# Two neighbouring blocks' short float32 products issued as one pair on the two column halves of TensorE

## What is computed

```python
x = _layernorm(x + _L0_gnn_ref(x, edge_index, ...), axis=-1)       # passes 0 and 1
# _L1_gnn_ref, passes 2 to 4:
def _mp_layer(x, src_f, dst_f, ea_f, W, b):
    m = jnp.concatenate([x[dst_f], x[src_f], ea_f], axis=1) @ W.T + b
    agg = jax.ops.segment_sum(m, dst_f, num_segments=n)
    return jax.nn.relu(agg)
h = _mp_layer(x, src_f, dst_f, ea_f, W0, b0)
h = jax.nn.relu(_batchnorm(h, g0, be0))
h = _mp_layer(h, src_f, dst_f, ea_f, W1, b1)
h = jax.nn.relu(_batchnorm(h, g1, be1))
h = _mp_layer(h, src_f, dst_f, ea_f, W2, b2)
x = _layernorm(x + h, axis=-1)
```

## Time and profile before

| | |
|---|---|
| median of 3 runs | 1153.56 us (1153.36 to 1153.74) |
| span of the profiled execution | 1151.4 us; its own time is not recorded apart, and the median lies 2.2 us above the span |
| TensorE busy (PE) | 973.9 us, 85% of the span |
| DVE busy | 718.9 us, 62% |
| ScalarE busy | 391.3 us, 34% |
| passes 2 to 4 | from 645.3 us to the end of the span |

### The profile page before, as it was taken

How to read it: one execution, slowest core, us unless ns; L and a number is a source line. 1 busy time by engine, 2 the same in 40 slices (tenths; PEclk the granted TensorE clock), 3 DMA queues, 4 the chain that set the end, 5 groups by cost and what they waited for, 6 DMA issues and landing times. The chain is left out here.

```text
span 1151.4 us, 19166 instructions
## 1 busy us (share of the span) xinstructions
PE 973.9 (85%) x7566; PEld 582.8 (51%) x7566; DVE 718.9 (62%) x1328; ACT 391.3 (34%) x750; POOL 131.4 (11%) x150
## 2 busy tenths in 40 slices
PE   0247877978688778999999999998999998999993
PEld 0246776868677665545555444443433443444441
DVE  5797989999999943623434755553465554334434
ACT  2485688887877720200000010213320104110000
POOL 4022223343222320000000000000000000000001
PEclk9868988989888977999999999998999998999997
DMA  6325546656545439953775435755036755037740
GB/s 165 57 74 206 177 130 242 199 177 195 174 125 181 177 127 292 377 235 140 317 278 211 183 120 234 276 219 224 15 126 249 286 192 224 19 147 280 286 173 23
DMA packets 63701, 216.77 MB, mean 188 GB/s; under 512 B 28320, under 2 KB 41627, under 8 KB 50067
## 3 DMA queue, kind: packets, MB, share of 16 engines
q1 hardware_dynamic: 55588, 164.52, 39.7%
q0 software_dynamic: 8016, 50.95, 12.3%
HBM read 170.69 MB, written 44.74 MB: 187 GB/s over the span
## 5 line engine op out<-in xcount | busy, mean ns | idle before, releaser
L1382 PE MATMUL PM<-Aring,Xop 128*128 128x512 fp8e4 (+1 forms) x1960 | 398.5, 363 | 0.0
L1382 PEld LDWEIGHTS PM<-Aring,Xop 128*128 128x128 f16 x1960 | 181.4, 98 | 216.7 <-issue 16.3
L821 PE MATMUL PW<-Aring 128*128 128x52 fp8e4 (+3 forms) x2151 | 120.9, 220 | 66.5 <-ACT F L889 64.0
L1907 ACT ACTIVATE F<-PH,bag 64x512 f32<-64x512 f32 (+1 forms) x39 | 25.5, 658 | 370.3 <-PE PH L1601 370.2
L821 PEld LDWEIGHTS PW<-Aring 128*128 128x128 fp8e4 x2151 | 114.8, 105 | 70.7 <-ACT F L889 66.5
L1382 PE MATMUL PM<-Ares,Xop 128*128 128x512 fp8e4 x588 | 138.1, 390 | 2.7 <-ACT Xop L1946 1.3
L1740 DVE TENSOR_SCALAR S<-PM 128x256 f32<-128x256 f32 (+1 forms) x75 | 31.4, 418 | 112.7 <-PE PM L1382 95.8
L1382 PEld LDWEIGHTS PM<-Ares,Xop 128*128 128x128 f16 x588 | 56.2, 100 | 71.7 <-issue 9.8
L1531 POOL DMA_DIRECT2D out<-dd x12 | 9.0, 754 | 705.8 <-DVE dd L1702 705.8
L889 ACT ACTIVATE F<-PW 128x392 uint16<-128x392 f32 x196 | 84.6, 513 | 11.0 <-PE PW L821 9.6
L679 DVE TENSOR_TENSOR Aring<-Ares 128x4096 uint16<-128x4096 uint16 x31 | 70.8, 2285 | 6.4 <-PE PW L821 6.1
(11 more groups left out here) (158 smaller groups left out, 1233.0 us busy)
## 6 DMA issues: line engine op xcount, KB each, us to landing
Aring<-adj SPq DMA_DIRECT2D x72, 1568.0 KB, 9.6
adj<-Aring POOLq DMA_DIRECT2D x12, 1568.0 KB, 5.9
adj<-Xop POOLq DMA_DIRECT2D x12, 1568.0 KB, 6.3
Ares<-adj SPq DMA_DIRECT2D x6, 1568.0 KB, 21.4
rc<-ea_sum SPq DMA_DIRECT2D x36, 128.0 KB, 5.7
Aring<-adj SPq DMA_DIRECT2D x4, 784.0 KB, 4.4
rc<-rc_d SPq DMA_DIRECT2D x12, 256.0 KB, 9.5
eaf<-in_erow SPq DMA_DIRECT2D x60, 51.0 KB, 2.0
```

What stands on the lines that cost most here:

```text
L821: last = nc.tensor.matmul(PW[begun % RING][:, c:c + 52 * (z - y)].rearrange("p (d v b) -> p d v b", d=z - y, b=2), lo[:, h % 2, i, :].bitc ...
L1382: last = nc.tensor.matmul(o, x[:, h, :], rhs, start=h == 0, stop=h == NT - 1)
L1907: nc.scalar.activation(F[0:64, c:c + w], PH[b % 2][0:64, 0:w], ACT.Relu, bias=t["bag"][:, 4 + conv:5 + conv]).then_inc(s_hr, 1)
```

## The change

In passes 2 to 4, `post(b)` of an even block does nothing (except the last, block 12), and `post(b)` of an odd block issues the short products of both, b-1 and b: first the two `ws` products, then the two `wc` products. The even block's output lies in partitions 0 to 63, the odd block's in 64 to 127 of one PSUM tensor, `PH[b // 2 % 2]`, so that the first uses TensorE's columns 0 to 63 and the second 64 to 127. ScalarE reads its half. In pass 4 the transposes follow three blocks behind instead of two, and ScalarE's `root(b-2)` stands ahead of the Relu of an even block. DVE, SP and GpSimd have the code that they had.

```diff
+        def halves(b):
+            return PH[b // 2 % 2][64 * (b % 2):64 * (b % 2) + 64, 0:blk(b)]
+
         def post(b):
             n, c = blk(b), b * 512
+            if p >= 2 and b % 2 == 0 and b < NB - 1:
+                return
             pe.wait_ge(s_S, b + 1)
             if p >= 2:
                 pe.wait_ge(s_r, b + 1)
...
             else:
-                if b >= 2:
-                    pe.wait_ge(s_hr, b - 1)
-                o = PH[b % 2][0:64, 0:n]
-                nc.tensor.matmul(o, m["ws"][conv][:], S[:, b % 2, 0:n], start=True, stop=False)
-                nc.tensor.matmul(o, m["wc"][conv][:], F[0:97, c:c + n], start=False, stop=True).then_inc(s_h, 1)
+                couple = [x for x in (b - 1, b) if x // 2 == b // 2]
+                if couple[0] >= 4:
+                    pe.wait_ge(s_hr, couple[0] - 2)
+                for x in couple:
+                    nc.tensor.matmul(halves(x), m["ws"][conv][:], S[:, x % 2, 0:blk(x)], start=True, stop=False)
+                for x in couple:
+                    nc.tensor.matmul(halves(x), m["wc"][conv][:], F[0:97, x * 512:x * 512 + blk(x)], start=False,
+                                     stop=True).then_inc(s_h, 1)
...
-        for i in range(NB + 2):
+        behind = 3 if p == 4 else 2
+        for i in range(NB + behind):
...
-            if i >= 2:
-                post2(i - 2)
+            if i >= behind:
+                post2(i - behind)
...
             else:
+                if p == 4 and b % 2 == 0 and 2 <= b < NB - 1:
+                    act.wait_ge(s_a, b - 1)
+                    root(b - 2)
                 act.wait_ge(s_h, b + 1)
-                nc.scalar.activation(F[0:64, c:c + w], PH[b % 2][0:64, 0:w], ACT.Relu,
+                nc.scalar.activation(F[0:64, c:c + w], PH[b // 2 % 2][64 * (b % 2):64 * (b % 2) + 64, 0:w], ACT.Relu,
                                      bias=t["bag"][:, 4 + conv:5 + conv]).then_inc(s_hr, 1)
-                if p == 4 and b >= 2:
+                if p == 4 and b >= 2 and (b % 2 or b == NB - 1):
                     act.wait_ge(s_a, b - 1)
                     root(b - 2)
```

## The result

The changed kernel takes 1180.74 us (1177.03 to 1181.79, 4 runs), the kernel before 1153.46: ratio 1.0228, 95% interval 1.0213 to 1.0243. The forecast was 1182.4, slower. The profiled execution took 1181.43 us, its span 1177.5. One execution each of the kernel before, of e10 and of e11 took far longer (1337, 1667 and 2556 us); the medians and ratios in this text leave them out.

The account below looks back on a forecast made before the run. TensorE bounds the kernel, with 1.8 us of slack for ring loads. Pass 2 +32.9, pass 3 -1.4, pass 4 -2.7 make +28.8 on the 1151.4 span: 1180.2, or 1182.4 by the median; range 1171 to 1206.

Parts of the forecast that it names:

- The move: Even blocks' products issued one main product later, so in pass 2 their check cannot begin under their own main product.
- The stalls: Pass 2: TensorE waits 8.7 us for ring loads ahead of blocks 6, 8 and 10; +22.3 us over the three.
- T_4: End of block 4's main product in a pass; in pass 2 no stall was forecast before it.
- The clock: Pass 2: lower clock behind each stall costs 2.2 us, +6.6 for three, and 1.0 more at the pass's end.
- The pair: Two blocks' short products on separate column halves take 2.28 us instead of 3.72, saving 1.44 where TensorE is the bound.
- instructions start in order: Within a pair, column halves overlap but starts keep program order: five slots instead of eight, 2.28 us.
- rival 5: Pair takes four slots, 1.86 us, 0.42 less than forecast: 4.6 us less in all, 1178; chance 0.18.
- T_10: End of block 10's main product in a pass; the forecast sums each pass's end from there.
- one microsecond to spare, no stall: Pass 3 steady part: ring load in at 25.0 us, wanted at 26.0, so TensorE does not stall.
- Rival 4: Pass 3 stalls too if loads land in 12.7 us: three of 1 us, +3, 1185; included in five slots' 0.48.
- The ends of passes: After block 10's main product: pass 2 +6.2 and 1 for clock, pass 3 +4.4, pass 4 +5.2 us.
- The number: Whole kernel: +28.8 us, span 1180.2, median 1182.4; slower with chance 0.92.

Follow-up runs that it names:

- e10: Changed kernel with DVE's check ahead of the statistics, blocks 10, 11, 12 and also blocks 0 and 1 of pass 3 issued one by one: 1129.23 us, ratio 0.9806.
- e11: Pairs in pass 4 only, passes 2 and 3 issuing each block's products singly as in the kernel before: 1149.89 us, ratio 0.9979.
- e1: Changed kernel with DVE's check moved ahead of the statistics in passes 2 and 3: 1138.85 us, ratio to the kernel before 0.9862.
- e2: Changed kernel with pairs shifted by one block (block 0 alone, then (1, 2) to (11, 12)), DVE's order untouched: 1199.93 us, ratio 1.0403.
- e9: Changed kernel with 36 unused products put in TensorE's queue ahead of main products 6, 8 and 10 of pass 2: 1173.95 us, ratio 1.0196.
- e3: Kernel of e1 with both blocks of a pair on columns 0 to 63: 1165.16 us, ratio to the kernel before 1.0100.
- e4: Kernel of e1 with products ordered block by block (A ws, A wc, B ws, B wc), column halves kept: 1137.42 us, ratio 0.9872.

## Why the prediction was right, point by point

- *The move.* Right, and the whole of the result. The check of an even block starts 3.3 us after its own main product and no longer under it; e1 and e2 show the cause from both sides.
- *The stalls.* 8.5, 9.6 and 8.6 us against 8.7 each (9.1 by its own times behind the longer check). From T_4 on, check, issue and landing are met within 0.2 us. That the first stall is too has some luck in it: the pair ended 0.4 us earlier than forecast, but main product 5 then waited 0.45 us for its own load, which stood behind `factors(4)` and so behind `sums(2)`. The prediction had costed that queue for a later load only, where it is hidden.
- *The clock.* Behind the three stalls 5.3 us (1.8, 1.5, 1.9) against 6.6; e9 shows that it is the clock. At the end of pass 2, where 1.0 was allowed, block 12's product took 4.19 us instead of 2.84 behind 3.3 us of idle. I counted the clock only in pass 2. It also met the first pair of pass 3, which had 5.0 us of idle ahead of it and took 3.5 us instead of 1.9 (granted clock 0.53), and the last pair of pass 4, which took 3.6 (0.50):

```profile
869.44 1.97 PE L1606 MATMUL PH<-S,ws 128*64 128x512 f32 x4 [5.02 <-DVE F L1757]
871.17 1.79 PE L1608 MATMUL PH<-F,wc 97*64 97x512 f32 x4
872.90 21.33 PE L1382 MATMUL PM<-Aring,Xop 128*128 128x512 fp8e4 x98
...
1149.67 1.98 PE L1606 MATMUL PH<-S,ws 128*64 128x512 f32 x4 [2.89 <-DVE S L1751]
1151.40 1.95 PE L1608 MATMUL PH<-F,wc 97*64 97x512 f32 x4
```

  I had the idle of the first down as 2.73 us with one set lying in it; the pair takes that set out of it, and the idle grows to 5.
- *The pair.* Wrong in size: 2.28 forecast, 1.87 measured. The step that failed is "instructions start in order"; rival 5 held, to which I gave 0.18. e3 shows that the halves are the reason, and e4 that four slots do not hang on the order in the program. It explains 0.4 of the 0.7 us by which T_4 came out lower (-3.9 for -3.2) and pass 4 until T_10 (-9.5 for -7.9; four pairs by 0.4).
  The Trainium skill, "TensorE: Matmul & The Clock Gate" (Packing small matmuls), has matmuls "pc-monotone in start AND end"; in e4 the starts did not keep the order of the program, and the measurement decides. By "TensorEngine Tiling (Array Packing)" (Key Properties) different tiles can execute in parallel, and by its Theoretical Speedup that gives up to 2x: here 3.58 / 1.87 = 1.9, it agrees.
- *Pass 3, "one microsecond to spare, no stall".* Wrong, for a queue that I had costed in pass 2 and at the end of pass 3 but not here: ScalarE's four sums over a round's check stand ahead of Relu(3), hence of the statistics of 3, hence of check(5):

```profile
896.13 0.68 ACT L1919 ACTIVATE F<-PH,bag 64x512 f32<-64x512 f32 x1 [21.75 <-PE PH L1608]
896.71 0.88 ACT L1889 ACTIVATE junk<-hT 128x832 uint8<-128x832 uint8 x1
...
900.77 0.69 ACT L1919 ACTIVATE F<-PH,bag 64x512 f32<-64x512 f32 x1
901.49 0.69 DVE L1828 BATCH_NORM_STATS2 bst<-F 64x6 f32<-64x512 f32 x1 [1.75 <-ACT F L1919]
902.10 0.57 DVE L1777 COPY hT<-Aring 128x1664 uint16<-128x1664 uint16 x1
...
909.82 0.79 SPq L1505 DMA_DIRECT2D Aring<-adj  x2
...
920.39 0.81 PE L1382 MATMUL PM<-Aring,Xop 128*128 128x512 fp8e4 x3 [1.16 <-issue]
```

  That was 1.75 us on DVE. The load of block 7 landed 1.2 us later than forecast, and the shorter pairs made TensorE want it 0.9 earlier; with the 1.0 to spare this gives the 1.2 us of idle. It was 2.1 more ahead of block 11, behind T_10. With the check first, 0.3 and 0.6 are left. Rival 4 had such stalls, but from slower loads; the loads took what they took.
- *The ends of passes.* Right in kind and near in size. I took the normalise stages as unchanged; they became 1.9 us shorter together. Over all the kernels here they take 66.9 to 68.9 us together; what that follows was not tried.
- *The number.* That it came so close is in part luck. In the span the forecast was 1180.2 and 1177.5 was measured. Pass 2 until T_10 (-2.5), the normalise stages (-1.9) and the pairs of pass 4 (-1.6) came out lower; pass 3 until T_10 (+1.2), the end of pass 4 (+1.5) and the stage before pass 2 (+0.6) higher. The median lies further above the span of the profile (3.2 us) than the 2.2 carried over, which leaves -1.7 of 1182.4. Rival 5, which had the pair right, gave 1178; the measured time lies above it because of the stalls of pass 3 and the clock outside pass 2, which neither sum had.

## What to carry to other kernels

When work is issued later, look not only at who needs its result but at what stands behind the waiting instruction in each queue: here a 0.7 us statistic held up a 7.6 us check, the check a 10.7 us load, and the load TensorE. A saving of 1.85 us a pair (two sets of 1.86 before, 1.87 now), real as it was, needed the consumers' queue put in the new order to show: 1180.7 us became 1138.9, and 1129.9 with the last blocks left single, 1.8% under the kernel before. Behind stalls like these of 8 to 10 us, add what the lower granted clock takes as well (here 1.5 to 1.9 us each, up to 2.8 in e2).

## What the runs showed of the hardware that was not expected

Float32 products on columns 0 to 63 and 64 to 127 run fully side by side: eight instructions in 1.87 us, 3.58 on the same columns. They do so even when one half's second product stands between them in the program (e4: 1.88 us, 664.22 to 666.10).

The length of an idle alone does not tell whether the clock falls. At the end of pass 4 TensorE idles 2.89 us ahead of the last pair in the changed kernel, in e1 and in e4, with the same work before it, and the pair then took 3.6, 2.9 and 1.9 us (granted clock 0.50 over the pair, 0.70 over its first 1.9 us, 1.00 over the pair). What decides between them was not tried.
